# The third MLP stage of a fused transformer block, computed with its features on the partitions

## The chip, the cores and the metric

The kernel runs on one core of one Trainium2 chip. The time is that of the whole launch on the device, in microseconds (us), and is given as the median of several runs. A profile comes from one more execution. PE is TensorE, ACT is ScalarE, DVE is VectorE, POOL is GpSimd and SP is SyncE, which here only issues DMAs.

## What is computed

The input x has 8 groups of 512 rows with 256 features. Cut to what matters, the reference is:

```
y = LN(x)                                   # no weights
y = y + attention(LN(y; ln1))               # causal linear attention, 64 features
y = y + f2(gelu(f1(LN(y; ln2))))            # 256 -> 1024 -> 256
x = x + y
z = LN(x)                                   # no weights
h = gelu(z @ ternary(W_fc).T)               # 256 -> 1024, weights -1, 0, 1
h = LN(h; ln_w, ln_b)                       # over the 1024 features
out = x + h @ ternary(W_proj).T             # 1024 -> 256, weights -1, 0, 1
```

The last four lines are the third stage, which the change rewrites. The kernel never forms the normalised h. With w for ln_w, mean mu and deviation r of a row of h, out is x + r·(W(w·h) − mu·W(w)) + W(ln_b): it projects w·h, and takes the mean off behind the projection with a row vector W(w), `csum_b` in the code. W(ln_b) is `cpj_b`.

## The kernel before

Work is done in groups g = 0 to 7 of N = 512 rows, four tiles t of 128. D is 256, the hidden width H is 1024. A matrix with features on the partitions has KD = 2 or KH = 8 blocks of 128, counted by m. A float32 value is kept as the sum of two rounded parts, hi and lo; a full product takes three matmuls (`split3`, L261), a product with exact ternary weights two. ACT writes the hi part from PSUM, DVE the lo part as PSUM − hi. PSUM has eight banks of 512 float32 per partition: bank_f (2), bank_y (2), bank_a (2), bank_p, bank_q.

Each engine runs a list of calls that is written out by hand (`first`, `step(g)`, `last` in each engine's block), and engines wait for each other's semaphores. Steps of up to three groups are interleaved. For a group they are:

- LN1 and attention: `tu`, `qk_mm`, `scores`, `v_mm`, `attend` on PE (L338 to L419), then LN2 and the transposes `tz2` (L421).
- `f1` (L428): eight calls m of six matmuls of 512 columns into bank_f[m % 2]; `gelu` (L758) on ACT in place, `h_hi` (L765) on ACT, `h_lo` (L1121) on DVE. `f2` (L450) adds 12 matmuls of 256 columns per m into bank_y, rows on the partitions; in the last group `f2h` (L461) does it by halves of the rows.
- LN3: `y_sum` (L1128), `ln3_stats` and the variance on DVE, `ln3_rstd` (a power) on POOL, `ln3_shift` on DVE, `z3_norm` on ACT, then the transposes `tz3` (L467), `z3_hi` (ACT), `z3_lo` (DVE).
- Stage 3: `fc(g, t, c)` (L477): rows on partitions, four matmuls of 512 columns into bank_f[c], eight calls. `gelu3` (L784) writes h into the SBUF buffer h3. `ln4_stats` (L1153) takes mean and variance per row on DVE with bn_stats. `tr(g, h, q)` (L494), eight calls, turns two blocks m of two tiles into bank_y[q % 2]. `g_hi` (L793, ACT) and `g_lo` (L1165, DVE) split them, scaled with w, 128x256 each. `proj` (L523, `last_proj` L508) takes 8 matmuls of 256 columns per call, two tiles (one half h) at a time into bank_p.
- `correct` (L1387, POOL) adds −mu·r·csum_b to yc, which holds x + cpj_b (`y_cpj`, L1377), and `output` (L1174, DVE) adds r times the projection. SP stores halves of a group.

The setup in the first 60 us loads and splits the weights, and finds the ternary ones (`threshold`, `ternary` L930).

## Time and profile before

| | us |
|---|---|
| median of 3 runs (lowest, highest) | 457.57 (457.09, 457.77) |
| span of the profiled execution | 455.2 |
| PE busy | 437.5 |
| DVE busy | 367.7 |
| ACT busy | 310.7 |
| POOL busy | 238.6 |

The span goes from the first to the last instruction of the profiled execution; its own time as a run is not listed, so the median stands beside it, 2.4 us longer. Instructions, DMA issues and waits are not counted as busy. A matmul's listed duration includes the pipeline behind it: two in a row overlap, and what one costs in the queue is read from start to start.

### The profile page before, as it was taken

The page shows a single profiled execution, that of the slowest core. Times are in us where ns is not written, and L with a number is a line of the kernel's source. Part 1 is how long each engine was busy: PE and PEld are TensorE (multiplying, and loading weights), DVE is VectorE, ACT ScalarE, POOL GpSimd, SP SyncE. Part 2 cuts the span into 40 slices and gives each one's busy share as a digit, 9 for nine tenths or more (in the row PEclk, how much of TensorE's full clock was granted, in tenths as well). Part 3 has the DMA queues.
Part 4 walks back from the last instruction along what each step waited for, and adds up shares of the span by engine and source line. Part 5 has one row for each costly group of instructions (what it writes and reads, how often), then busy time and mean ns, then how long its engine had stood idle before and what let it go on. Part 6 is the DMA issues. An engine that isn't in the chain of part 4 may idle for free.

```text
span 455.2 us, 8867 instructions
## 1 busy us (share of the span) xinstructions
PE 437.5 (96%) x2942; PEld 395.5 (87%) x2942; DVE 367.7 (81%) x1200; ACT 310.7 (68%) x580; POOL 238.6 (52%) x224
## 2 busy tenths in 40 slices
PE   3898999999989999999999999999999999999997
PEld 3786897889978899889998999889988899888986
DVE  6899989877968878888788879888799837867596
ACT  4887937895188855878668855779468854786173
POOL 3887215843358517682549525694496225181334
PEclk9999999999999999999999999999999999999999
DMA  7234010120111201030101201021100000000001
GB/s 241 118 99 181 0 49 1 48 71 1 9 62 48 69 3 48 34 102 6 48 25 48 69 2 46 25 70 48 48 24 1 24 1 1 25 1 24 0 25 48
DMA packets 13518, 20.41 MB, mean 45 GB/s; under 512 B 2720, under 2 KB 11040, under 8 KB 12960
## 3 DMA queue, kind: packets, MB, share of 16 engines
q1 hardware_dynamic: 13472, 19.84, 13.3%
q8 instruction: 24, 0.39, 0.3%
q14 instruction: 22, 0.18, 0.1%
HBM read 15.62 MB, written 4.22 MB: 44 GB/s over the span
## 4 chain that ended last, share of the span: by engine, by line
PE 76%; DVE 7%; issue 7%; POOL 4%; DMA 3%; ACT 1%; SPq 1%; POOLq 0%; DVEq 0%
PE bank_f L490 11%; PE bank_p L538 10%; PE bank_f L263 6%; PE bank_f L265 6%; PE bank_f L264 6%; PE bank_y L263 6%; PE bank_y L264 6%; PE bank_y L265 6%; PE bank_y L504 5%; PE bank_a L263 4%; PE bank_a L265 4%; PE bank_a L264 4%; DMA h<-in_f 2%; PE bank_a L271 1%; PE bank_f L271 1%
## 5 line engine op out<-in xcount | busy, mean ns | idle before, releaser
L1334 POOL TENSOR_TENSOR rs<-ve,neg_half 128x2 f32<-128x2 f32 x48 | 33.6, 702 | 134.1 <-DVE ve L972 131.2
L763 ACT ACTIVATE bank_f<-bank_f,f_bias 128x512 f32<-128x512 f32 x64 | 42.3, 660 | 37.8 <-PE bank_f L265 36.9
L263 PE MATMUL bank_y<-wf_hi,h_hi 128*128 128x256 f32 x240 | 67.2, 280 | 0.0
L264 PE MATMUL bank_y<-wf_lo,h_hi 128*128 128x256 f32 x240 | 67.1, 280 | 0.0
L265 PE MATMUL bank_y<-wf_hi,h_lo 128*128 128x256 f32 x240 | 67.1, 279 | 0.0
L1035 DVE TENSOR_TENSOR h_lo<-bank_f,h_hi 128x512 fp32r<-128x512 f32 x60 | 41.3, 688 | 29.9 <-ACT h_hi L771 29.5
L1170 DVE SCALAR_TENSOR_TENSOR g_lo<-bank_y,vec,g_hi 128x256 fp32r<-128x256 f32 x128 | 55.5, 478 | 10.7 <-ACT g_hi L800 10.2
L800 ACT ACTIVATE g_hi<-bank_y,vec 128x256 fp32r<-128x256 f32 x128 | 53.4, 479 | 12.0 <-PE bank_y L504 10.3
L538 PE MATMUL bank_p<-wpj_t,g_hi 128*128 128x256 f32 x240 | 60.0, 286 | 0.0
L538 PE MATMUL bank_p<-wpj_t,g_lo 128*128 128x256 f32 x240 | 58.6, 280 | 0.0
L263 PE MATMUL bank_f<-z2T_hi,wf_hi 128*128 128x512 f32 x128 | 52.4, 410 | 3.0 <-DVE h_lo L1035 1.9
L490 PE MATMUL bank_f<-wfc_t,z3T_hi 128*128 128x512 f32 x128 | 53.8, 420 | 0.6 <-DVE z3T_lo L1035 0.6
L265 PE MATMUL bank_f<-z2T_hi,wf_lo 128*128 128x512 f32 x128 | 50.8, 397 | 0.0
L490 PE MATMUL bank_f<-wfc_t,z3T_lo 128*128 128x512 f32 x128 | 50.6, 395 | 0.0
L264 PE MATMUL bank_f<-z2T_lo,wf_hi 128*128 128x512 f32 x128 | 50.6, 395 | 0.0
L791 ACT ACTIVATE h<-bank_f 128x512 f32<-128x512 f32 x64 | 38.6, 604 | 14.5 <-PE bank_f L490 13.5
L263 PEld LDWEIGHTS bank_y<-wf_hi,h_hi 128*128 128x128 f32 x240 | 45.1, 188 | 1.3 <-issue 0.3
L538 PEld LDWEIGHTS bank_p<-wpj_t,g_hi 128*128 128x128 f32 x240 | 45.1, 188 | 1.1
L538 PEld LDWEIGHTS bank_p<-wpj_t,g_lo 128*128 128x128 f32 x240 | 45.2, 188 | 1.1
L264 PEld LDWEIGHTS bank_y<-wf_lo,h_hi 128*128 128x128 f32 x240 | 45.1, 188 | 1.0
L265 PEld LDWEIGHTS bank_y<-wf_hi,h_lo 128*128 128x128 f32 x240 | 45.1, 188 | 0.0
L1156 DVE BATCH_NORM_STATS2 bn<-h 128x6 f32<-128x512 f32 x64 | 40.9, 681 | 0.0
(299 smaller groups left out, 1227.7 us busy)
## 6 DMA issues: line engine op xcount, KB each, us to landing
out<-y_yc SPq DMA_DIRECT2D x15, 256.0 KB, 2.2
u<-in_xt SPq DMA_DIRECT2D x6, 512.0 KB, 3.7
lines_b<-lines SPq DMA_DIRECT2D x6, 512.0 KB, 3.9
x_even<-in_x SPq DMA_DIRECT2D x8, 256.0 KB, 2.9
x_odd<-in_x SPq DMA_DIRECT2D x8, 256.0 KB, 3.1
h<-in_f SPq DMA_DIRECT2D x1, 1024.0 KB, 7.7
y_yc<-in_f SPq DMA_DIRECT2D x1, 1024.0 KB, 10.0
h<-in_fc SPq DMA_DIRECT2D x1, 1024.0 KB, 4.8
```

What stands on the lines that cost most here:

```text
L263: pe.matmul(ps, w[0], r[0], start=start, stop=False, skip_group_check=skip)
L264: pe.matmul(ps, w[0], r[1], start=False, stop=False, skip_group_check=skip)
L265: return pe.matmul(ps, w[1], r[0], start=False, stop=stop, skip_group_check=skip)
L490: mm = pe.matmul(bank_f[c][:], z3T[part][:, k, t * P:(t + 1) * P], wfc[:, k, c * 512:(c + 1) * 512], start=(k == 0 and part == 0), stop=(k ...
L538: mm = pe.matmul(bank_p[:, t * D:(t + 1) * D], gr[part][:, (8 * g + 4 * h + q) % RG, i, t * P:(t + 1) * P], wpj[:, m, :], start=(m == 0 an ...
L763: act.activation(bank_f[m % 2][:], bank_f[m % 2][:], ACT.Gelu, bias=f1_bias[:, m:m + 1]).then_inc(s["h_gelu"], 1)
L791: act.activation(h3[:, t, c * 512:(c + 1) * 512], bank_f[c][:], ACT.Gelu).then_inc(s["h3_ready"], 1)
L800: act.activation(gr[0][:, n % RG, i, :], bank_y[q % 2][:, i * D:(i + 1) * D], ACT.Copy, scale=ln3w_c[:, m:m + 1]).then_inc(s["g_hi"], 1)
L1035: dve.tensor_tensor(dst, b, hi.bitcast(F32), ALU.subtract).then_inc(s[ready], 1)
L1156: dve.bn_stats(bn[3][:, t, 6 * c:6 * c + 6], h3[:, t, c * 512:(c + 1) * 512]).then_inc(s["ln4_bn"], 1)
L1170: dve.scalar_tensor_tensor(gr[1][:, n % RG, i, :], bank_y[q % 2][:, i * D:(i + 1) * D], ln3w_c[:, m:m + 1], gr[0][:, n % RG, i, :].bitcast ...
L1334: pool.tensor_tensor(rs[n][:, 2 * h:2 * h + 2], ve[n][:, 2 * h:2 * h + 2], neg_half[:, 0:2], ALU.pow).then_inc(s[f"ln{n + 1}_rs"], 1)
```

## The change

Stage 3 keeps its features on the partitions from fc to proj.

- `fc(g, m)` takes the weights block m as the stationary operand and moves the 512 rows: bank_f[m % 2] then holds features m by rows. For m = 0 and 1 it is cut into halves of 256 rows (`fch`), and so is f1 (`f1h`). No transpose of h is needed.
- `gelu3` works in place in PSUM. ACT's `g_hi` and `square` and DVE's `g_lo` (which waits for both) read the bank from there, 512 columns each.
- `proj(g, m)` moves 258 columns: the weights block of 256, and two more that hold 1/w as hi and lo. A tile's 257th and 258th results add up to the sum of h over the features. Its four tiles lie in bank_y[0], bank_y[1], bank_p and bank_a[0], so f2 of the next group waits for `centre`.
- POOL adds the eight squared blocks (`sq_add`, seven per group), PE transposes the sum (`tsq`), DVE sums over it (`h2_sum`).
- DVE makes mean and variance from the two sums (`h_sum`, `ln4_var`) and takes the mean off each tile (`centre`); POOL does rstd once per group and `output` (two multiplications, two additions); in the last group DVE's `last_output`.
- 1/w needs w ≠ 0: where w is 0, 1 is used in its place and the row of the projection weights is masked (`used_weights` on DVE, `wpj_mask` on POOL, `inv_hi` and `inv_lo`).
- All call lists are written anew, one `order()` per engine; the stores of SP come half 1 before half 0 in groups 1 to 4 and 6.

The core of it, with one row of the lists:

```diff
-        wpj = sb("wpj_t", [P, KH, D], F32R)
+        wpj = sb("wpj_t", [P, KH, D + 2], F32R)
...
+        def out_bank(t):
+            return (bank_y[0], bank_y[1], bank_p, bank_a[0])[t]
...
+            def fc_wait(g, m):
+                if g == G - 1 and m < 2:
                     pe.wait_ge(s["h_lo"], 8 * G)
...
+                if m >= 2:
+                    pe.wait_ge(s["g_lo"], 8 * g + m - 1)
+                    pe.wait_ge(*squared(g, m - 2))
+
+            def fc_mm(m, cols):
                 for k in range(KD):
                     for part in range(2):
-                        mm = pe.matmul(bank_f[c][:], z3T[part][:, k, t * P:(t + 1) * P], wfc[:, k, c * 512:(c + 1) * 512],
+                        mm = pe.matmul(bank_f[m % 2][:, cols], wfc[:, k, m * P:(m + 1) * P], z3T[part][:, k, cols],
                                        start=(k == 0 and part == 0), stop=(k == KD - 1 and part == 1))
...
+            def proj(g, m):
+                pe.wait_ge(s["g_lo"], 8 * g + m + 1)
...
+                for t in range(T):
+                    for part in range(2):
+                        mm = pe.matmul(out_bank(t)[:, 0:D + 2], gr[part][:, (8 * g + m) % RG, t * P:(t + 1) * P],
+                                       wpj[:, m, :], start=(m == 0 and part == 0), stop=(m == KH - 1 and part == 1))
...
+            def tsq(g):
...
+                for t in range(T):
+                    mm = pe.transpose(bank_a[1][:, t * P:(t + 1) * P], squares[:, 0, t * P:(t + 1) * P], ident[:])
...
+            def gelu3(g, m):
+                act.wait_ge(s["fc_done"], 8 * g + m + 1)
+                act.wait_ge(s["fc_half"], 2 * g + min(m, 1) + 1)
+                act.activation(bank_f[m % 2][:], bank_f[m % 2][:], ACT.Gelu).then_inc(s["h3_ready"], 1)
...
+            def square(g, m):
...
+                act.activation(squares[:, m, :], bank_f[m % 2][:], ACT.Square).then_inc(squared(g, m)[0], 1)
...
+            def g_lo(g, m):
+                n = 8 * g + m
+                dve.wait_ge(s["g_hi"], n + 1)
+                dve.wait_ge(*squared(g, m))
...
+            def h_sum(g):
...
+                for t in range(T):
+                    dve.wait_ge(s["pj_tile"], 4 * g + t + 1)
+                    dve.tensor_reduce(h_total[:, t:t + 1], out_bank(t)[:, D:D + 2], AXX, ALU.add).then_inc(s["h_total"], 1)
...
+                dve.scalar_tensor_tensor(centred[:, t, :], csum_b, h_mean[:, t:t + 1], out_bank(t)[:, 0:D],
+                                         ALU.mult, ALU.add).then_inc(s["centred"], 1)
...
+            def sq_add(g, m):
...
+                pool.tensor_tensor(squares[:, 0, :], squares[:, 0, :], squares[:, m, :], ALU.add).then_inc(s["squares_sum"], 1)
...
+                f2(7, 6, 0); f2(7, 7, 0); f2(7, 5, 1); f2(7, 6, 1); f2(7, 7, 1); tz3(7, 0); tz3(7, 1); fch(7, 0, 0)
```

Three places of the engines' queues follow. Names left of the arrow are written, those right of it read. The first is PE at the seam of group 2, where v_mm of group 3 (into bank_a from wvo) ends and the transposes tz3 of group 2 (into bank_f from z) begin; L538 is proj, v_hi and ae_hi belong to attend. Before:

```order
L265 MATMUL bank_a<-wvo_hi,uT_lo 128x256
L538 MATMUL bank_p<-wpj_t,g_hi 128x256
L538 MATMUL bank_p<-wpj_t,g_lo 128x256
...
L263 MATMUL bank_a<-v_hi,ae_hi 128x258
L265 MATMUL bank_a<-v_hi,ae_lo 128x258
L538 MATMUL bank_p<-wpj_t,g_hi 128x256
L538 MATMUL bank_p<-wpj_t,g_lo 128x256
...
L263 MATMUL bank_a<-v_hi,ae_hi 128x258
...
L271 MATMUL bank_f<-ident,z 128x128 x4
```

And with the change:

```order
L287 MATMUL bank_a<-wvo_lo,uT_hi 128x256
L288 MATMUL bank_a<-wvo_hi,uT_lo 128x256
L294 MATMUL bank_f<-ident,z 128x128 x8
L286 MATMUL bank_a<-v_hi,ae_hi 128x258
L287 MATMUL bank_a<-v_lo,ae_hi 128x258
...
L288 MATMUL bank_a<-v_hi,ad_lo 128x258
L519 MATMUL bank_f<-z3T_hi,wfc_t 128x256
L519 MATMUL bank_f<-z3T_lo,wfc_t 128x256
```

The proj calls between v_mm and the transposes are gone, and both tz3 come directly behind v_mm, ahead of attend(3, 0) and attend(3, 1), after which the first fc halves (L519) follow.

The second is ACT at the start of stage 3 of the same group. Before (h is the gelu's result in SBUF):

```order
L791 ACTIVATE h<-bank_f 128x512
L662 ACTIVATE z<-xa,sh,rs 128x256 x2
L791 ACTIVATE h<-bank_f 128x512 x3
L800 ACTIVATE g_hi<-bank_y,vec 128x256 x2
L756 ACTIVATE z2T_hi<-bank_a 128x2x256
L791 ACTIVATE h<-bank_f 128x512
L800 ACTIVATE g_hi<-bank_y,vec 128x256 x2
L791 ACTIVATE h<-bank_f 128x512
```

With the change (h now holds the squares, bank_f<-bank_f is the gelu):

```order
L805 ACTIVATE z3T_hi<-bank_f 128x2x256 x2
L765 ACTIVATE v_hi<-bank_a 128x2x256
L810 ACTIVATE bank_f<-bank_f 128x512
L824 ACTIVATE g_hi<-bank_f,w_used 128x512
L836 ACTIVATE h<-bank_f 128x512
L810 ACTIVATE bank_f<-bank_f 128x512
L836 ACTIVATE h<-bank_f 128x512
L824 ACTIVATE g_hi<-bank_f,w_used 128x512
L716 ACTIVATE uT_hi<-u 128x2x256
L810 ACTIVATE bank_f<-bank_f 128x512
```

Gelu no longer leaves the bank; each m has three ops on it, and the copies and squares stand in alternating order.

The third is DVE at the end of the program. Before:

```order
L1170 SCALAR_TENSOR_TENSOR g_lo<-bank_y,vec,g_hi 128x256 x2
L978 TENSOR_SCALAR sh<-mv,rs 128x1 x2
L972 TENSOR_SCALAR ve<-mv 128x1 x2
L1170 SCALAR_TENSOR_TENSOR g_lo<-bank_y,vec,g_hi 128x256 x4
L978 TENSOR_SCALAR sh<-mv,rs 128x1 x2
L1170 SCALAR_TENSOR_TENSOR g_lo<-bank_y,vec,g_hi 128x256 x4
L1184 SCALAR_TENSOR_TENSOR y_yc<-bank_p,rs,y_yc 128x256 x2
L1184 SCALAR_TENSOR_TENSOR y_yc<-bank_a,rs,y_yc 128x256 x2
```

With the change:

```order
L1263 SCALAR_TENSOR_TENSOR g_lo<-bank_f,w_used,g_hi 128x512 x8
L1221 TENSOR_REDUCE h_total<-bank_a 128x4
L1231 TENSOR_REDUCE h_total<-bank_y 128x1 x2
...
L1236 SCALAR_TENSOR_TENSOR h_mean<-h_total 128x4
L1241 SCALAR_TENSOR_TENSOR ve<-h_total,h_mean 128x4
L1243 TENSOR_SCALAR ve<-ve 128x4
L1251 TENSOR_SCALAR h_mean<-h_total 128x4
L1256 SCALAR_TENSOR_TENSOR centred<-pj_rows_b,h_mean,bank_y 128x256 x2
L1256 SCALAR_TENSOR_TENSOR centred<-pj_rows_b,h_mean,bank_p 128x256
L1271 SCALAR_TENSOR_TENSOR y_yc<-centred,rs,y_yc 128x256 x2
L1256 SCALAR_TENSOR_TENSOR centred<-pj_rows_b,h_mean,bank_a 128x256
L1271 SCALAR_TENSOR_TENSOR y_yc<-centred,rs,y_yc 128x256 x2
```

Statistics stood among the g_lo steps; now the sums, the variance and the centring all follow the last g_lo, and the outputs close the queue.

## Rows read from the trace of the kernel before

**Rows 1.** Page, busy time, share of the span and instructions of each engine
```profile
PE 437.5 (96%) x2942; PEld 395.5 (87%) x2942; DVE 367.7 (81%) x1200; ACT 310.7 (68%) x580; POOL 238.6 (52%) x224
```

**Rows 2.** Stretches: us, busy and instructions by engine, clock, DMA share, GB/s
```profile
0.00:72.30 72.30, 60.18 (x375) 52.33 (x375) 63.16 (x202) 50.61 (x90) 37.10 (x41) 1.00 0.31 108
...
180.04:231.90 51.86, 51.86 (x360) 47.64 (x358) 42.87 (x145) 37.30 (x69) 29.87 (x27) 1.00 0.13 42
...
430.00:455.20 25.20, 21.85 (x152) 19.56 (x151) 19.26 (x58) 12.28 (x26) 9.25 (x9) 1.00 0.10 33
```

**Rows 3.** Waits: engine, out, line, releaser: us, times, longest
```profile
PE bank_a L279 <- DVE less_w L891: 7.1, 1, 7.1
```

**Rows 4.** Timeline of PE, stage 3 of group 2: start, us, engine, line, operation
```profile
185.22 0.60 PE L504 MATMUL bank_y<-ident,h 128*128 128x128 f32 x4
185.58 0.48 PE L490 MATMUL bank_f<-wfc_t,z3T_hi 128*128 128x512 f32 x1
185.90 0.40 PE L490 MATMUL bank_f<-wfc_t,z3T_lo 128*128 128x512 f32 x1
186.13 0.39 PE L490 MATMUL bank_f<-wfc_t,z3T_hi 128*128 128x512 f32 x1
```

**Rows 5.** Groups by form: count, busy us and mean ns, idle before
```profile
L504 PE MATMUL bank_y<-ident,h 128*128 128x128 f32 x256 | 37.8, 272 | 0.0
L1156 DVE BATCH_NORM_STATS2 bn<-h 128x6 f32<-128x512 f32 x64 | 40.9, 681 | 0.0
L800 ACT ACTIVATE g_hi<-bank_y,vec 128x256 fp32r<-128x256 f32 x128 | 53.4, 479 | 12.0 <-PE bank_y L504 10.3 <-PE bank_p L538 1.6
L1396 POOL TENSOR_TENSOR y_yc<-y_yc,mean_part 128x512 f32<-128x512 f32 x16 | 20.9, 1303 | 1.2
L708 ACT ACT_TABLE_LOAD x7 | 9.0, 1283 | 0.1
```

**Rows 6.** Timeline of PE, 256 and 258 columns, first and twelfth call
```profile
213.02 0.28 PE L263 MATMUL bank_y<-wf_hi,h_hi 128*128 128x256 f32 x1
...
214.32 0.28 PE L265 MATMUL bank_y<-wf_hi,h_lo 128*128 128x256 f32 x1
...
230.08 0.28 PE L263 MATMUL bank_a<-v_hi,ae_hi 128*128 128x258 f32 x1
...
231.42 0.28 PE L265 MATMUL bank_a<-v_hi,ad_lo 128*128 128x258 f32 x1
```

**Rows 7.** Timeline of ACT, stage 3 and f1 of the middle
```profile
185.42 0.60 ACT L791 ACTIVATE h<-bank_f 128x512 f32<-128x512 f32 x1 [0.77 <-PE bank_f L490]
185.91 0.84 ACT L800 ACTIVATE g_hi<-bank_y,vec 128x256 fp32r<-128x256 f32 x2
...
195.06 0.66 ACT L763 ACTIVATE bank_f<-bank_f,f_bias 128x512 f32<-128x512 f32 x1 [0.27 <-PE bank_f L265]
195.75 0.60 ACT L771 ACTIVATE h_hi<-bank_f 128x512 fp32r<-128x512 f32 x1
```

**Rows 8.** Timeline of DVE and ACT after group 7's last f2 half
```profile
430.49 0.69 DVE L1136 TENSOR_TENSOR y_yc<-bank_y,y_yc 128x512 f32<-128x512 f32 x1 [0.84 <-PE bank_y L265]
...
433.38 0.34 DVE L978 TENSOR_SCALAR sh<-mv,rs 128x1 f32<-128x1 f32 x2 [0.81 <-POOL rs L1334]
...
433.79 0.60 ACT L662 ACTIVATE z<-y_yc,sh,rs 128x256 f32<-128x256 f32 x1 [0.84 <-DVE sh L978]
```

**Rows 9.** Timeline of the last DVE step, and of a 128x4 rstd on POOL
```profile
451.55 0.88 DVE L1184 SCALAR_TENSOR_TENSOR y_yc<-bank_a,rs,y_yc 128x256 f32<-128x256 f32 x2 [0.15 <-POOL y_yc L1396]
...
202.25 1.04 POOL L1328 TENSOR_TENSOR rs<-ve,neg_half 128x4 f32<-128x4 f32 x1
```

**Rows 10.** Timeline of DVE in the setup, and a group of small ones
```profile
39.60 1.73 DVE L939 TENSOR_SCALAR y_yc<-h,theta 128x1024 f32<-128x1024 f32 x1
...
48.13 0.74 DVE L939 TENSOR_SCALAR y_yc<-h,theta 128x1024 f32<-128x1024 f32 x1
...
L956 DVE TENSOR_SCALAR few_rows<-mean_w,select 4x128 f32<-4x128 f32 x2 | 1.5, 774 | 0.0
```

More of the change, by code:

```diff
@@ L325, in cpj @@
                 for k in range(KH):
[L326 removed]
+                    mm = pe.matmul(bank_p[0:4, 0:D], ln3_split[:, k, :], wpj[:, k, 0:D],
                                    start=(k == 0), stop=(k == KH - 1))
@@ L533, in proj @@
                         pe.wait_ge(s["spread_ready"], 1)
-                for i in range(2):
-                    m = 2 * q + i
-                    for t in range(2):
-                        for part in range(2):
-                            mm = pe.matmul(bank_p[:, t * D:(t + 1) * D],
-                                           gr[part][:, (8 * g + 4 * h + q) % RG, i, t * P:(t + 1) * P], wpj[:, m, :],
-                                           start=(m == 0 and t == 0 and part == 0), stop=(m == KH - 1 and part == 1),
-                                           skip_group_check=True)
@@ L604, in _ @@
+            order()
         @block.scalar
@@ L861, in _, with pj_wait @@
-            first()
-            for g in range(1, 4):
-                step(g)
-            last()
+            def gelu3(g, m):
+                act.wait_ge(s["fc_done"], 8 * g + m + 1)
+                act.wait_ge(s["fc_half"], 2 * g + min(m, 1) + 1)
+                act.activation(bank_f[m % 2][:], bank_f[m % 2][:], ACT.Gelu).then_inc(s["h3_ready"], 1)
+            def pj_wait(n):
+                act.wait_ge(s["pj_tile" if n % KH == 0 else "pj_done"], n // KH * 4 if n % KH == 0 else n - n // KH)
@@ L866, in _ @@
+            order()
         @block.vector
@@ L1261, in _, with h2_sum @@
-            first()
-            for g in range(1, 4):
-                step(g)
-            last()
+            def h2_sum(g):
+                dve.wait_ge(s["sq_done"], g + 1)
+                if g:
+                    dve.wait_ge(s["ln4_ve"], g)
+                dve.tensor_reduce(h2_total[:], bank_a[1][:].rearrange("p (t f) -> p t f", t=T),
+                                  AXX, ALU.add).then_inc(s["h2_total"], 1)
+            def h_sum(g):
+                if g:
+                    dve.wait_ge(s["h_mean"], g)
+                    dve.wait_ge(s["h_mean2"], g)
+                for t in range(T):
+                    dve.wait_ge(s["pj_tile"], 4 * g + t + 1)
+                    dve.tensor_reduce(h_total[:, t:t + 1], out_bank(t)[:, D:D + 2], AXX, ALU.add).then_inc(s["h_total"], 1)
@@ L1266, in _ @@
+            order()
         @block.gpsimd
```

777 lines of the change are left out of this document (420 added, 357 removed).

## The prediction

> **What bounds the kernel now.** I read the page's busy times first. TensorE (PE) is busy 437.5 of 455.2 us; the others have a fifth to a half of the span to spare [rows 1]. Then the table by stretch, to see whether that holds everywhere. In the middle it does: a group takes 51.9 us and PE is busy for all of it, at a granted clock of 1.00 (2.4 GHz), while DVE, ACT and POOL work 42.9, 37.3 and 29.9 us of it. Of PE's 17.7 idle us, 12.1 lie in the first 72.3 us and 3.35 in the last 25.2 [rows 2]; 2.3 are left for all between. So in the middle only PE work counts, and a wait for another engine costs nothing until it is longer than the matmuls that the order puts beside it. Most of the idle time at the start is one wait for the setup weights, 7.1 us [rows 3], which the change leaves.
>
> **What leaves PE.** The stretch of rows inside a group shows what a transposing call of stage 3 costs in the queue. Its four transposes start at 185.22 and the next matmul at 185.58, which then takes .32 us to the following start instead of .23: .36 + .09, so .44 us [rows 4]. Eight calls a group (256 transposes in all [rows 5]) are 3.5 us a group. The new tsq(g), four transposes of the squares' sum, brings one such call back: −.44. The projection keeps 64 matmuls a group, now 258 columns wide. Twelve calls of 256 columns go .118 us apart ((214.32 − 213.02)/11), twelve of 258 columns .122 ((231.42 − 230.08)/11) [rows 6]; that would be .26 us a group. Two columns at the pace of a 512-column matmul, .23/512, are .06 us a group. I take .13, between the two. The fc matmuls keep their columns: 32 × 512, or 24 × 512 and 16 × 256 where m = 0 and 1 are cut in halves, at the same pace per column within .01 us. Net 2.95 us a group, 23.6 us in all. PE work falls from 437.5 to 413.9 us, 48.9 per group.
>
> If nothing else changed, that alone would give 457.57 − 23.6 = 434 us. The rest of this part is what takes it back.
>
> **The other engines.** DVE loses bn_stats (64 in 40.9 us) and some small steps, and 128 g_lo of 256 columns become 64 of 512; it falls to about 35 us a group. ACT has 64 gelu (.66), 64 scaled copies (.69 at most) and 64 squares (.60) of 512 columns for 64 gelu (.60) and 128 copies (.48, 53.4 in all) [rows 5, 7]: 125 for 92 us, 4.1 a group more, some 41 us. In the queue it is less per op: two independent ops of 512 columns start .49 us apart, an op that needs the one before it .69 us after it [rows 7]. With about .09 more for a scale column (an estimate from those two) gelu, copy and square take .65 + .57 + .50, near 1.7 us per m. POOL gains seven adds of 128x512 (the kind of L1396, 1.30 us each [rows 5]), and its four correction steps become four output steps: 29.9 + 9.1, 39 us. SP's stores and loads change places, but all DMAs use 13% of the engines in a group [rows 2], and the steps that refill yc have a whole group's time: nothing. All three stay under 48.9, so none bounds by its sum.
>
> **The new chain inside stage 3.** The third stage now works in two PSUM banks in turn. In each, the next fc may start only when the bank was read by g_lo and square: fc .93, some .20 to the release, gelu .65, copy .57, square .60 where it starts late, g_lo .69 and .1 to PE. That is 3.75 us per bank and round, 1.87 us per m, 15 us for eight. In the same stretch PE has 16.4 us of work (fc 7.5, seven proj at .98, tz2 and part of attend), so on paper it is covered. But the cover is uneven: the first two m have only attend beside them, and ACT also has z2_norm and z2_hi there. Nothing in the trace prices this. The bounds are nothing (covered) and 1.87 (one m exposed); I charge a third of that, .6 us a group, as the cover is 1.4 us in all: 4.2 for seven groups. Before, a bank was free after gelu alone, and transposes and proj lay between.
>
> **The seam between f2 and fc.** Before, in the order, proj(g−1) and attend stood between v_mm and tz3; now proj is done earlier, and in groups 1 and 2 tz3 comes straight after v_mm. The chain after the last f2 can be read in the last group: y_sum starts at 430.49, released by the f2 that ended some .2 before; statistics, variance and POOL's rstd follow, the shift ends at 433.72 and ACT's z at 434.39 [rows 8], 4.1 us in all. v_mm is 24 matmuls, 2.9 us, and v_hi stands before z3_norm on ACT (.4 more), so tz3 is late by some 1.6 us in groups 1 and 2; with one or two attends (.4 to .7 us) in between, .5 in groups 3 to 6, and in group 0 (v_mm, cpj and spread first) .2. Sum 5.4. The start of f2 now waits for centre(g−1), because proj's results lie in f2's banks: after the last proj some 3 us of sums and centre steps on DVE, beside it 2.8 us of f1(g, 2) and (g, 3); .3 a group, 2.1. Two masks of wpj on POOL, 2.6 us each by L1396's pace, stand before the first proj and may cost nothing or 2.6: 1, as fc lies beside them. Groups 0 to 6 idle 12.7 us, where they idled 2.3.
>
> **Start.** selectors, ln3_lo and the ternary steps stand elsewhere on DVE and the first scores after v_mm. A gain of 4 us and a loss of 1 are the bounds, since the 7.1 us wait stays: I take 2, 10 us idle.
>
> **The end.** Before, the last f2 ends at about 430.3 [rows 8] and the span 24.9 us later, with PE nearly full, because f2 half 0 was finished first and fc already ran. Now f2(7,7,1) closes the queue for tz3(7,1), and nothing stands behind it. Counted from the last f2: z at 4.1, tz3 to 4.5, z3_hi 5.1, z3_lo 5.8; half 0 is through earlier and its half of fc runs in that wait, as if the whole fc had started at 5.3. With fc .93 and .2 the first gelu starts at 6.4, the eighth seven rounds of 1.87 later, at 19.5. Its gelu and square (1.25) and POOL's add (1.3) end at 22.2 with the hand-over; tsq(7) and then the last proj follow on PE, 1.8 us with releases: 24.0. Then four sums, mean and variance (1.0), rstd of 128x4 on POOL 1.04 us [rows 9], and one centre step and the four outputs behind it (five of .44): 28.4. From the last DVE op's end to the span's end went 2.8 us (451.55 + .88 = 452.43 [rows 9]); that makes 31.2. PE works 16.4 us of it and idles 14.8.
>
> **Sum.** 413.9 + 10 + 12.7 + 14.8 = 451.4 us of span. The three runs before have a median of 457.57, 2.4 over the profiled span; adding the same, **453.8 us**. The removal is worth 23.6 us, and all but 3.8 is given back.
>
> **A rule against the change.** POOL is to be busy for 39 of 49 us a group. Its work seems to slow DVE ops that read SBUF alone: the compare of 128x1024 took 1.73 us at 39.60 and .74 at 48.13, and ops of 4x128 average .77 us [rows 10]. h_mean, the variance and the first small sums are such ops. The Trainium skill, "GPSIMD Engine Reference", section "Key points", says that POOL shares its SBUF interfaces with VectorE and contends with DVE instructions in a 2-port mode or with two SBUF inputs. By that rule, centre and f2 behind it would come later, which is the third case below; the sum above has no charge for it.
>
> **Rivals and chances.** A measurement of this kernel can tell about 0.2% from no change, 456.7 to 458.5 us.
> - *Stalls take most of it* (my forecast, 449 to 456.6), 0.45.
> - *The stalls are covered.* PE is full at 51.9 us with the orders as they stand, so a new order may well be full too [rows 2]. Groups 0 to 6 would idle 4, the start 12, the end 14.8: 413.9 + 30.8 + 2.4 = 447.1. Against it: the bank now waits for three readers. 0.15.
> - *Contention by POOL.* Four small DVE ops per group at .7 in place of .15 us are 2.2 us in the chain to centre, of which matmuls of f1 may hide three quarters; .5 us a group shows, 4 in all, giving 457.8, no change. 0.15.
> - *The two-bank round sets the pace* (slower). If ACT reaches each bank .2 us later than I assume (a z2_norm or u_hi in front, a square that cannot start beside the copy), four rounds a bank add .8 us a group, 8 groups 6.4 us: 460.2. For it: 1.87 against a PE supply of 2.05 us per m is a cover of a tenth only, and tz2, z2_norm and z2_hi fall into it. Against: ACT had 14 us free per group [rows 2]. From .47 us more per group than I charged (3.8/8) the gain is gone, and from .59 the change is slower by over 0.2%. 0.25.
> - *Square needs a table of its own.* A load takes 1.28 us [rows 5]; two for each of 64 m are 160 us on ACT. The program's order holds 14 loads on ACT, before 16, so I leave it no chance.
>
> The range takes in the covered case but for its tail, and the last case up to a little over its centre, so that some 0.1 of it is left out: 446 to 461.5 us; faster 0.60, same 0.15, slower 0.25.
>
> **What would show it.** Right: PE's busy time near 414 and, per middle group, 1.5 to 2.5 us of PE idle time, released by g_lo or square (fc, f1) and z3_lo; the stretch from the last f2 to the end near 31 us with PE busy about half of it. Covered: a period of 49 us. Contention: h_mean and ve of .6 us or more, PE waiting for centred. Rounds: PE waits for g_lo at nearly every fc, period over 51.9. Wrong altogether: DVE or POOL with no idle time in a group, or PE's busy time near 437, which would mean that the pitch of 258 columns or of the wide matmuls is not as read here; or a granted clock under 1.00, which would raise every PE term.

## The result: 468.8 us, slower by 2.3%

| | before | after |
|---|---|---|
| median of 4 runs (lowest, highest), us | 457.67 (457.09, 459.0) | 468.8 (466.49, 469.22) |
| span of the profiled execution | 455.2 | 467.3 |
| its own time | not listed | 469.05 |

The ratio is 1.0233, with a 95% interval of 1.0205 to 1.0262. The forecast of 453.8 us and its range both miss, and on the wrong side. The page of the changed kernel, its busy times and PE's clock in 40 slices:

```profile
PE 428.6 (92%) x2878; PEld 386.6 (83%) x2878; DVE 327.9 (70%) x1027; ACT 329.3 (70%) x579; POOL 306.5 (66%) x270
...
PEclk9899899999999999999999999999999999999799
```

PE is busy 8.9 us less than in [rows 1], not 23.6. That number deceives: a matmul's listed duration holds the pipeline behind it, so that after each wait some idle time is listed as busy, and at half clock a matmul is listed longer (.41 us in place of .28 for 256 columns). I therefore give every matmul its pitch from start to start at full clock (.2335 us for 512 columns, .117 for 256, .120 for 258, .109 for a transpose), and call the sum **PE's work** and all else **idle**. Work is 425.0 us before and 402.2 after: 22.8 us were removed, as forecast (23.6). The idle time by stretch:

| PE idle, us | before | after | more | forecast |
|---|---|---|---|---|
| start to the first fc (72.3; 78.7) | 20.1 | 27.2 | +7.1 | −2.1 |
| from there to the end of the last f2 (430.3; 434.3) | 6.0 | 21.4 | +15.4 | +10.4 |
| from there to the end (24.9 us; 33.0 us) | 4.2 | 16.6 | +12.4 | +11.4 |

(The forecast counted its idle time against PE's listed busy time; the column gives its differences to [rows 2] as it read them: 12.1, 2.3 and 3.35.) Together 34.9 us are lost and 22.8 gained: +12.1, the 467.3 − 455.2 of the spans. (The median is 1.5 us over the span here and was 2.4 over it before, so the medians differ by 11.1.) The stretches of the changed kernel (us, busy time and instructions by engine, clock, DMA share, GB/s) are the start, one middle group, and the end, as in [rows 2]:

```profile
0.00:78.70 78.70, 61.36 (x382) 53.94 (x382) 63.12 (x208) 47.84 (x89) 41.42 (x44) 0.96 0.30 100
183.40:237.00 53.60, 52.22 (x359) 47.13 (x358) 38.20 (x122) 39.78 (x70) 38.97 (x34) 1.00 0.13 41
434.30:467.30 33.00, 20.66 (x118) 17.43 (x116) 16.09 (x43) 16.48 (x29) 16.18 (x14) 0.86 0.10 33
```

No engine is full. The granted clock, 1.00 in all of [rows 2], is .96 and .86 in two of these stretches. (The trace has no clock record before 12.1 us in the kernel before and 11.2 in the changed one, and the views count that time as 1.00. PE goes at half pace there in both: the transposes from 7.99 on are .21 us apart in the kernel before, twice their pitch.)

**The start.** PE's and DVE's timelines (start us, us, engine, line, operation, idle before and releaser):

```profile
18.55 0.77 PE L286 MATMUL bank_p<-uT_hi,wqk_hi 128*128 128x512 f32 x1 [4.32 <-DVE wqk_lo L924]
48.98 0.79 PE L286 MATMUL bank_f<-z2T_hi,wf_hi 128*128 128x512 f32 x1 [2.27 <-DVE h_lo L1101]
```

```profile
13.79 0.75 DVE L1051 BATCH_NORM_STATS2 bn<-x_odd 128x6 f32<-128x256 f32 x2 [4.71 <-DMA x_odd<-in_x]
...
15.05 1.28 DVE L1106 SCALAR_TENSOR_TENSOR uT_lo<-bank_f,uT_hi 128x512 fp32r<-128x512 f32 x2
16.25 2.16 DVE L924 SCALAR_TENSOR_TENSOR wqk_lo<-qk_relu,vec,wqk_hi 128x128 fp32r<-128x128 f32 x2
```

DVE's new list puts ln1_stats(1, 0), which needs a DMA, ahead of u_lo and wqk_lo, which the first qk product needs: that product starts at 18.55, against 12.45 before. In the stretch behind the gap PE runs at half clock:

```profile
18.50:21.40 2.90, 2.85 (x7) 2.30 (x8) 1.94 (x9) 0.60 (x1) 2.82 (x4) 0.50 0.00 0
```

The second gap above, 2.3 us ahead of 48.98, has half clock about its end again, from 48.7 to 52.1. There PE waits for an h_lo that stands on DVE behind two ternary steps, 3.5 us together (44.74 to 48.2); before, the same pair of steps left PE a gap of 1.41 us. The loss of 7.1 us is nearly made up of these: a gap of 4.3 us that was not there, .9 more in the second, and about 1.4 us of pace lost in each half clock stretch, less the .9 us by which PE's first product comes sooner.

**The middle.** PE's waits (us in total, times, longest), of which before knew only the second, with 1.7 us:

```profile
PE bank_f L519 <- DVE g_lo L1263: 6.6, 11, 1.0
...
PE bank_f L294 <- ACT z L683: 5.7, 7, 3.1
...
PE bank_y L286 <- DVE centred L1256: 0.7, 2, 0.4
```

The second includes the 3.1 us ahead of the last group's end. The same waits end PE's weight loads too, so some more is hidden under PEld. By what came next after an excess over the pitch, the five periods from 130.5 to 392.3 lose 8.2 us ahead of or inside fc, 3.5 at the seam (tz3 2.3, attend 1.2), 2.6 in f2, 1.2 in f1, 1.1 in scores and proj. A period is 52.4 us: 49.0 of work and 3.3 idle. Before it was 52.1: 51.6 and .5.

**The end.** The wait ahead of tz3(7, 0) is 3.08 us, and then the clock is halved:

```profile
437.52 0.84 PE L294 MATMUL bank_f<-ident,z 128*128 128x128 f32 x4 [3.08 <-ACT z L683]
438.62 1.09 PE L294 MATMUL bank_a<-ident,z 128*128 128x128 f32 x4 [0.26 <-DVE z L1082]
439.87 0.55 PE L519 MATMUL bank_f<-z3T_hi,wfc_t 128*128 128x256 f32 x1 [0.16 <-DVE z3T_lo L1101]
440.21 0.41 PE L519 MATMUL bank_f<-z3T_lo,wfc_t 128*128 128x256 f32 x1
440.43 0.41 PE L519 MATMUL bank_f<-z3T_hi,wfc_t 128*128 128x256 f32 x1
```

fc's 256 columns are .21 us apart here; in the middle .12. The table by stretch:

```profile
437.80:444.70 6.90, 5.74 (x24) 4.44 (x22) 2.41 (x4) 4.02 (x8) 1.79 (x2) 0.51 0.23 80
```

### The profile page after: what moved, and what is told of

Its sections match the earlier page's. It is cut to its first block and busy times, and to the rows that moved or that the text cites. A ratio compares the mean times of both kernels' runs of the same rounds, so it can differ in the third digit from the quotient of the medians.

```text
span 467.3 us, 8905 instructions
## 1 busy us (share of the span) xinstructions
PE 428.6 (92%) x2878; PEld 386.6 (83%) x2878; DVE 327.9 (70%) x1027; ACT 329.3 (70%) x579; POOL 306.5 (66%) x270
## 5 line engine op out<-in xcount | busy, mean ns | idle before, releaser
L1443 POOL TENSOR_TENSOR h<-h 128x512 f32<-128x512 f32 x56 | 72.4, 1292 | 14.9 <-issue 7.5
L1263 DVE SCALAR_TENSOR_TENSOR g_lo<-bank_f,w_used,g_hi 128x512 fp32r<-128x512 f32 x64 | 47.9, 749 | 46.2 <-ACT h L836 24.4
L519 PE MATMUL bank_f<-z3T_hi,wfc_t 128*128 128x512 f32 (+1 forms) x160 | 58.6, 379 | 7.1 <-DVE g_lo L1263 6.6
L286 PE MATMUL bank_f<-z2T_hi,wf_hi 128*128 128x512 f32 (+1 forms) x160 | 57.9, 362 | 3.4 <-DVE h_lo L1101 2.5
L288 PE MATMUL bank_f<-z2T_hi,wf_lo 128*128 128x512 f32 (+1 forms) x160 | 56.4, 352 | 0.0
L287 PE MATMUL bank_f<-z2T_lo,wf_hi 128*128 128x512 f32 (+1 forms) x160 | 56.3, 352 | 0.0
L519 PE MATMUL bank_f<-z3T_lo,wfc_t 128*128 128x512 f32 (+1 forms) x160 | 55.0, 355 | 0.0
L810 ACT ACTIVATE bank_f<-bank_f 128x512 f32<-128x512 f32 x64 | 37.7, 589 | 11.8 <-PE bank_f L519 11.0
L824 ACT ACTIVATE g_hi<-bank_f,w_used 128x512 fp32r<-128x512 f32 x64 | 43.8, 687 | 1.3 <-PE bank_a L548 0.4
L519 PEld LDWEIGHTS bank_f<-z3T_hi,wfc_t 128*128 128x128 f32 x160 | 31.1, 194 | 15.8 <-DVE g_lo L1263 11.8
```

The source lines that it names most:

```text
L286: pe.matmul(ps, w[0], r[0], start=start, stop=False, skip_group_check=skip)
L287: pe.matmul(ps, w[0], r[1], start=False, stop=False, skip_group_check=skip)
L288: return pe.matmul(ps, w[1], r[0], start=False, stop=stop, skip_group_check=skip)
L519: mm = pe.matmul(bank_f[m % 2][:, cols], wfc[:, k, m * P:(m + 1) * P], z3T[part][:, k, cols], start=(k == 0 and part == 0), stop=(k == KD ...
L810: act.activation(bank_f[m % 2][:], bank_f[m % 2][:], ACT.Gelu).then_inc(s["h3_ready"], 1)
L824: act.activation(gr[0][:, n % RG, :], bank_f[m % 2][:], ACT.Copy, scale=w_used[:, m:m + 1]).then_inc(s["g_hi"], 1)
```

## Experiments

Each ratio is to the kernel before, run beside that version on the same chip (medians 456.9 to 457.67), so differences of some tenths between rows of the table mean nothing. Each run's idle time is from its own profiled execution, by the pitches above: start to the first fc; the first fc of group 0 to that of group 6; the end from the last f2 (the whole length, in brackets the idle time in it; the filling of e4_fill counts as work).

| run | median, us | ratio, 95% interval | start | middle | end |
|---|---|---|---|---|---|
| before | 457.67 | | 20.1 | 5.6 | 24.9 (4.2) |
| the change | 468.8 | 1.0233, 1.0205–1.0262 | 27.2 | 19.7 | 33.0 (16.6) |
| b1_nocover | 468.65 | 1.0253, 1.0236–1.027 | 19.7 | 17.8 | 25.0 (4.2) |
| b2_tail | 464.07 | 1.0149, 1.0125–1.0172 | 20.7 | 5.6 | 31.3 (10.5) |
| e1_start | 466.32 | 1.019, 1.0158–1.0222 | 22.9 | 19.6 | 34.8 (18.4) |
| e5_setup | 467.25 | 1.0228, 1.0212–1.0243 | 25.5 | 19.2 | 33.2 (16.8) |
| e9_setup2 | 464.65 | 1.0169, 1.0145–1.0192 | 22.3 | 20.0 | 33.2 (16.7) |
| e4_fill | 467.32 | 1.0227, 1.0202–1.0253 | 26.8 | 19.4 | 33.5 (14.3) |
| e6_tail | 473.24 | 1.0352, 1.0304–1.0399 | 27.0 | 19.9 | 35.1 (19.0) |
| e2_nosq | 460.29 | 1.0047, 1.0015–1.0078 | 27.4 | 17.0 | 32.1 (16.1) |
| e8_noadd | 466.6 | 1.0207, 1.0192–1.0222 | 26.3 | 18.5 | 33.0 (16.6) |
| e3_sqsb | 477.8 | 1.0477, 1.0409–1.0545 | 26.3 | 26.1 | 34.3 (17.8) |
| e11_gfirst | 469.28 | 1.027, 1.025–1.0291 | 26.2 | 20.1 | 34.4 (17.9) |
| e12_z2dve | 472.37 | 1.0311, 1.0292–1.033 | 23.8 | 25.2 | 33.3 (16.9) |
| e13_z2none | 465.75 | 1.0177, 1.0147–1.0208 | 23.7 | 19.7 | 33.1 (16.7) |
| e14_z2nosq | 457.81 | 1.0018, 1.0002–1.0034 | 22.3 | 18.4 | 31.2 (15.2) |

### The start: e1_start, e5_setup, e9_setup2

e1_start, in DVE's list:

```diff
-                u_odd(0, 1); ln1_stats(1, 0); u_lo(0, 0)
-                u_lo(0, 1); wqk_lo(); qk_bias_add(); wvo_add(); ln1_stats(1, 1)
+                u_odd(0, 1); wqk_lo(); qk_bias_add(); u_lo(0, 0)
+                u_lo(0, 1); ln1_stats(1, 0); wvo_add(); ln1_stats(1, 1)
```

> Only DVE's list is changed: ln1_stats(1, 0) comes behind wqk_lo, qk_bias_add and the two u_lo of group 0. After the change DVE waited 4.7 us for x_odd there, with these steps queued behind it, PE's first qk product started at 18.55 us in place of 12.45, and PE's clock stood at half from 18.0 to 21.4 us. If this queue is the loss at the start, the qk product starts near 14 to 14.5, that stretch of half clock is gone, and the time falls by 4 to 6 us, to 463 to 465. Rival: the start is bound by the weights' arrival and by the later waits (h_lo at 48.98), and less than 1.5 us come back.

The first qk product started at 13.87, the first fc came at 74.4, 4.3 us sooner, and the first half clock stretch was gone; the second stayed (45.0 to 48.4). The time fell by only 2.5 us, between what was expected and the rival: behind the last f2 the clock stayed at half from 434.1 to 444.4, 3.4 us longer than in the change, for no edit there.

e5_setup puts the calls of all engines up to tz3(0, ·) in the old kernel's order; e9_setup2 besides moves two calls of POOL:

```diff
-                n1o(1); ln1_rstd(2, 0); ln1_rstd(2, 1); x_mul(2, 0); ln3_rstd(0, 0)
-                ln3_rstd(0, 1); x_mul(2, 1)
+                n1o(1); ln1_rstd(2, 0); ln1_rstd(2, 1); ln3_rstd(0, 0); ln3_rstd(0, 1)
+                x_mul(2, 0); x_mul(2, 1)
```

> The change with the setup's call lists of before on PE, DVE, ACT and POOL, up to the second v_mm of group 1 (used_weights and inv_hi added among them, one gelu_table call more); from tz3(0, 0) on everything as with the change. If the order of the setup alone makes its start late, the first fc comes at 72 to 73 us in place of 78.7, no stretch of half clock is left before 60 us, and the time is 462 to 463.5. Rival: the new work of the setup (used_weights, halves of f1) costs some of it, and the first fc comes at 75 or later; then 465 or more.

> As e5_setup (the setup's lists of before), and on POOL the two ln3_rstd of group 0 stand ahead of x_mul(2, 0). In e5_setup PE came to tz3(0, 0) 6 us sooner, at 68.6 us, and then waited 4.6 us: POOL's x_mul(2, 0) waited for its DMA until 69.5 and took 1.5, with ln3_rstd behind it. If the loss at the start is only which step stands behind a wait for a DMA, the first fc comes at 72 to 73.5, the half clock at 73.4 is gone, and the time falls to 462 to 463.5. Rival: another wait takes its place, and the time stays over 465.

e5_setup brought PE to tz3 of group 0 some 6 us sooner, where it lost most of that again, so that the first fc came at 77.0 and the time was the rival's, though not for the rival's reason. PE and POOL in it:

```profile
73.26 2.10 PE L294 MATMUL bank_f<-ident,z 128*128 128x128 f32 x8 [4.46 <-ACT z L719]
```

```profile
69.54 1.51 POOL L1500 TENSOR_TENSOR u<-u,lines_b 128x512 f32<-128x512 f32 x1 [7.35 <-DMA lines_b<-lines]
```

x_mul(2, 0) waited 7.4 us for a DMA with ln3_rstd(0, ·) queued behind it, and z of group 0 needs that rstd. With the two changed round (e9_setup2) the first fc comes at 73.8, and 4.1 us of the change's 11.1 are back, about 1 us less than was expected. In the change itself the x_mul cost nothing yet, since everything was late already: it was through at 69.9, and the ln3_rstd behind it then waited for DVE.

```profile
73.55 0.71 POOL L1419 TENSOR_TENSOR rs<-ve,neg_half 128x2 f32<-128x2 f32 x1 [3.61 <-DVE ve L1038]
```

So of the 7.1 us that PE idles more at the start, 4.9 are order, with the clock that dropped in the gaps: ln1_stats(1, 0) in front of what the first qk product needs (e1_start), then the rest of the setup's lists. x_mul in front of ln3_rstd is a second trap that shows once the first is gone. The other 2.2 us stay in e9_setup2, which waits 1.8 us at tz3 of group 0; their cause was not tested.

### The cover at the seam: b1_nocover

The kernel before with three calls of proj a group moved ahead of the last f2, as the changed kernel must do it (its results lie in f2's banks). No work is added:

```diff
-                scores(g + 2); f2(g + 1, 4); f1(g + 1, 7)
+                scores(g + 2); proj(g, 1, 1); proj(g, 1, 2); proj(g, 1, 3); f2(g + 1, 4); f1(g + 1, 7)
...
-                v_mm(g + 2, 0); v_mm(g + 2, 1); proj(g, 1, 1)
-                attend(g + 2, 0); proj(g, 1, 2); attend(g + 2, 1); tz3(g + 1, 0)
+                v_mm(g + 2, 0); v_mm(g + 2, 1)
+                attend(g + 2, 0); attend(g + 2, 1); tz3(g + 1, 0)
```

> The kernel before, with one edit of PE's list: in groups 2 to 6 the three proj calls of the group before (1, 1) to (1, 3) that stood between v_mm and fc stand behind scores instead, ahead of the rest of f1 and f2. Nothing else changes, no work is added. If those calls cover the LN3 chain, PE waits .6 to 1.5 us at tz3 and fc in each of five groups, and the time rises by 3 to 7 us, to 460 to 464: that much of the change's loss in the middle would be the lost cover. If v_mm and attend cover the chain alone, the time stays within 1 us of 457.5.

It is as slow as the change, which is chance: it has all of the old PE work and none of the losses at the start and the end. It is also 5 us slower than was expected. PE's waits in it; the first was 1.7 us in the kernel before, the third .6, the second not among the listed:

```profile
PE bank_f L271 <- ACT z L662: 3.6, 7, 0.6
PE bank_a L263 <- DVE v_lo L1035: 3.1, 2, 2.2
PE bank_f L490 <- DVE z3T_lo L1035: 2.1, 5, 0.6
```

The middle idles 12.2 us more: 1.3 to 1.9 in each of three groups, which is near what was expected, and 4.6 and 2.5 in the last two, where attend waits for v_lo and the clock falls once (342.0 to 345.4). So the chain from f2 to fc was there before, hidden in part behind these 24 matmuls (2.8 us). The other engines' lists were left as they were, and the v_lo part comes of lists that were made for the other order. The change, whose lists were made for its own order, loses far less at this place (3.5 us in five groups), so this run shows that the calls were cover; it does not say what their loss cost the change.

### Stage 3, ACT or POOL: e2_nosq, e8_noadd, e12 to e14

e2_nosq leaves out squares, their sum and its transposes, and makes the variance from a constant. e8_noadd leaves out POOL's adds alone.

```diff
             def square(g, m):
+                return
...
             def sq_add(g, m):
+                return
```

> Leaves out the squares: ACT's square, POOL's sq_add and PE's tsq are gone, the sum of squares is a constant. The four transposes of tsq are .44 us a group, 3.5 in all. If the two-bank round of stage 3 (gelu, copy, square, g_lo) makes PE's idle time in the middle (2.9 us a group over that of before, by start to start), a round is .5 to .6 us shorter per bank, the middle period falls from 52.4 to about 50 us, and the last round takes about 1.4 us per m in place of 1.94 (4 us less at the end); in all 468.8 falls by 3.5 + 8 + 4, to 451 to 455. If the idle time comes from elsewhere (seams, the order, DVE), only tsq and some of the end come back: 461 to 465.

> Leaves out POOL's sq_add alone (the variance is then that of one block's squares): ACT still squares and g_lo, fc and f1 still wait for it, tsq still runs. 9 us of POOL work per group are gone. If POOL's load slows DVE's small SBUF ops and so the start of f2, h_mean (128x4) falls from .43 to .17 us at the median, ve likewise, and 1 to 3 us come back (466 to 468). If the bank's readers on ACT and DVE are all that counts, nothing comes back before the last group, and the end gains at most .5 us: 468 to 469.

Without squares ACT has 4.8 us less a group (eight of .595), and idles 2.6 to 4.3 us between the first and the eighth gelu, where it idled .6 to .75 in five of groups 1 to 6. Yet PE's idle time in the middle falls by 2.7 us of 19.7 only. The time, 460.29 us, is just under what was expected if the two-bank round is not the cause (461 to 465). The span is 7.4 us shorter: 3.5 of PE work, the 2.7, 1.1 ahead of the last group's end and .5 in it, less .2 at the start. Without the adds alone the middle gains 1.2 us; of the 2.2 us in all, .9 lie in the start, which this edit leaves alone, so that the 466.6 fits the expectation for POOL's load in its time, but only about half of it in its place.

e12_z2dve (with e9_setup2's start) moves the odd tiles of z2 from ACT to DVE, as z2_odd behind ln2_shift in DVE's list; e13_z2none writes one column of them; e14_z2nosq is e13 and e2 together, so both leave work out.

```diff
-                pair(z, xa, 1, h, 0, "z2_ready", g == 0)
+                pair(z, xa, 1, h, 0, "z2_ready", True)
```

> The start order of run e9_setup2, and besides in every group the two odd tiles of the second norm (z2, [128x256] scaled and shifted by ACT, about .5 us each) are computed by DVE, so that some 1.0 us of ACT's work per group leaves the stretch in which ACT is also to serve gelu, copy and square. DVE gets 1.0 us per group more, with room for it. Theory A (ACT paces stage 3, since it is busy for all but .7 us of it): the stretch from the first to the eighth gelu falls from about 15.2 to 14.3 to 14.8 us and the idle time of PE between the groups falls by 2 to 5 us; time 460 to 463 (e9_setup2: 464.65). Theory B (PE's queue without cover, or the hand-over of the two banks, sets the pace and ACT's being busy is a result of it): the groups keep a period near 52.3 us, PE idles as before; time 464 to 465.5.

> As e12_z2dve, but the two odd tiles of the second norm are left out in groups 1 to 7 (DVE writes one column of each, some .15 us), so the stage behind them reads old values there; ACT has 1.0 us less per group, DVE nothing more. Theory A (ACT's work paces stage 3): first to eighth gelu 14.1 to 14.4 us against 15.2, PE's idle time in the middle 3 to 6 us below e9_setup2's 20.0, time 459 to 462. Theory B (the hand-over through DVE's g_lo and the banks paces it): stage 3 stays within .3 us of 15.2, ACT idles over 1.5 us in it, time 464 to 465.5. Theory C (the order lacks cover elsewhere: f2, tz3, attend): stage 3 gets shorter, but PE's idle time turns up elsewhere, middle idle falls by under 2 us, time 463 to 464.5.

> As e13_z2none, and the squares, their sum and its transposes are left out too (the variance is made from a constant), as in e2_nosq: ACT has 5.8 us less per group than the change, POOL 9 us less. Theory A: PE stalls in fc nearly vanish, the middle idles under 12 us (e2_nosq 17.0, e9_setup2 20.0), time 452 to 455. Theory C: what is left idle does not depend on ACT's or POOL's work, the middle keeps 15 to 18 us as in e2_nosq, time 456 to 459 (e2_nosq 460.29 with the slower start, some 3 us).

e12_z2dve was 7.7 us slower than e9_setup2, 5.2 of it in the middle: outside both expectations. DVE's group of z2_odd and PE's wait for g_lo:

```profile
L1153 DVE TENSOR_SCALAR z<-xa,rs,sh 128x256 f32<-128x256 f32 x16 | 13.8, 862 | 0.6
```

```profile
PE bank_f L518 <- DVE g_lo L1336: 11.9, 19, 1.2
```

Each is .86 us on DVE, twice a group, ahead of a g_lo that PE waits for; in e13_z2none, with the same relief for ACT and none of this, the row reads

```profile
PE bank_f L518 <- DVE g_lo L1340: 6.6, 12, 1.2
```

like that of the change. There ACT idles 1.1 to 1.7 us in stage 3 (2.8 in group 2), but the stage lasts 15.1 to 15.5 us as before (16.8 in group 2, as before too) and the middle idles 19.7: theory A falls, and of the other two it is theory B that had a stage of the same length. e14_z2nosq bears out that A falls: its time (457.81) is in the range of theory C, its middle (18.4) just over it (15 to 18). B and C are not told apart by these runs; they name the same waits from two sides, the bank's way back and the place in PE's queue where nothing lies beside it. The middle in the change, and in it:

```profile
78.70:392.30 313.60, 305.04 (x2100) 277.36 (x2099) 224.45 (x713) 238.66 (x416) 224.94 (x193) 1.00 0.11 35
```

```profile
73.80:383.40 309.60, 301.44 (x2076) 274.64 (x2075) 220.24 (x720) 211.23 (x356) 173.21 (x152) 1.00 0.12 35
```

ACT works 27 and POOL 52 us less, and PE still idles 18.4 against 19.7 us. What PE loses in the middle hangs on neither engine's sum of work. What is left is the chains that PE's queue leaves uncovered; no run gave the changed kernel its cover back, so this is read from the trace. They show one by one: the fc of m = 2, the first that needs a bank back, starts .43 to 1.07 us late in five of groups 1 to 6, since attend alone lies between (in group 2 it is a later fc, 1.17). Group 4 of the change:

```profile
291.96 0.28 PE L288 MATMUL bank_a<-v_hi,ad_lo 128*128 128x258 f32 x1
293.15 0.50 PE L519 MATMUL bank_f<-z3T_hi,wfc_t 128*128 128x512 f32 x1 [0.91 <-DVE g_lo L1263]
...
295.15 0.40 PE L519 MATMUL bank_f<-z3T_hi,wfc_t 128*128 128x512 f32 x1
```

From there on, fc and proj fill PE for 1.9 us per m. ACT's gelu, copy and square take 1.76 to 1.78 back to back (the gelu at 298.94 to the next at 300.72), but the second norm's z and z2T_hi and the next group's uT_hi stand among them, and together they leave ACT only .6 to .75 us idle: the two engines are level.

### The bank's readers: e3_sqsb, e11_gfirst

e3_sqsb squares g_hi from SBUF in place of the bank, with g_hi ahead of square in ACT's list, so that fc no longer waits for square. The sum is then that of other squares than the reference's. e11_gfirst is the order alone.

```diff
-                act.activation(squares[:, m, :], bank_f[m % 2][:], ACT.Square).then_inc(squared(g, m)[0], 1)
+                act.wait_ge(s["g_hi"], 8 * g + m + 1)
+                act.activation(squares[:, m, :], gr[0][:, (8 * g + m) % RG, :].bitcast(F32), ACT.Square).then_inc(squared(g, m)[0], 1)
```

> ACT's square reads the copy g_hi in SBUF (so it squares w times h) in place of the bank, and stands behind the copy everywhere; fc, f1 and g_lo no longer wait for it. ACT, POOL and PE do the same work as with the change, but a bank has two readers behind gelu. If the serial readers of the bank make the stalls, 5 to 9 us come back (460 to 464), nearly as much as the squares' removal gives beyond tsq. If ACT's own work (1.8 us per m) is the pace, nearly nothing comes back at the end (last round still 1.9 us per m) and under 3 us in all (466 to 468).

> The change with ACT's copy g_hi ahead of the square for every m (27 of 64 pairs swapped), all waits kept. e3_sqsb had this order and read the square from SBUF, and was 9 us slower than the change. If the order did that (the square then delays g_lo and the next gelu at the wrong places), this one is slower too, 472 to 478. If reading the square from SBUF did it, this one is within 2 us of 468.8.

The miss of the study: 9 us slower, where a reader less should have helped. ACT in the last group of e3_sqsb:

```profile
452.11 0.69 ACT L822 ACTIVATE g_hi<-bank_f,w_used 128x512 fp32r<-128x512 f32 x1
452.91 0.63 ACT L835 ACTIVATE h<-g_hi 128x512 f32<-128x512 f32 x1
453.45 0.58 ACT L808 ACTIVATE bank_f<-bank_f 128x512 f32<-128x512 f32 x1
```

The square starts .80 us behind the copy whose result it needs, .11 after its end; an independent op follows .50 to .59 behind. That is some .2 us for each m; the first to the eighth gelu take 16.0 to 17.7 us in place of 14.9 to 16.8, and the middle idles 6.4 us more. So ACT's pace stands just at PE's: taking work off ACT brings little, adding to it costs at once. The order alone costs nothing that can be told (469.28 against 468.8).

### The end: e4_fill, e6_tail, b2_tail

e4_fill puts 12 matmuls of 512 columns, whose result nobody reads, into the last gap; e6_tail finishes half 0 of the last group first, as the old kernel did; b2_tail takes that head start from the kernel before, on PE and ACT (shown: PE).

```diff
-                f2(7, 7, 1); tz3(7, 0); tz3(7, 1); fch(7, 0, 0)
+                f2(7, 7, 1); keep(12); tz3(7, 0); tz3(7, 1); fch(7, 0, 0)
```

```diff
-                f2(7, 6, 1); f2(7, 7, 1); tz3(7, 0); tz3(7, 1); fch(7, 0, 0)
-                fch(7, 0, 1); fch(7, 1, 1); fch(7, 1, 0)
+                f2(7, 6, 1); tz3(7, 0); f2(7, 7, 1); fch(7, 0, 0); fch(7, 1, 0); tz3(7, 1)
+                fch(7, 0, 1); fch(7, 1, 1)
```

```diff
-                f2h(7, 7, 1); fc(7, 0, 0); fc(7, 0, 1); proj(6, 1, 2); fc(7, 1, 0); proj(6, 1, 3); tz3(7, 1)
+                f2h(7, 7, 1); tz3(7, 1); fc(7, 0, 0); fc(7, 0, 1); proj(6, 1, 2); fc(7, 1, 0); proj(6, 1, 3)
```

> Twelve matmuls of 512 columns on operands at hand, into bank_p, stand between the last f2 and tz3(7, 0), where PE idled 3.1 us and the granted clock then fell to half from 437.85 to 444.7 us. If the idle time is what lets the clock fall, it stays at 1.00 there; the transposes and the first fc halves take half the time, the first gelu starts about 1.8 us sooner after the last f2, and the time falls by 1.5 to 2 us, to about 467. Rival: the clock falls anyway, or the fill delays tz3; then no gain or a loss of up to .5.

> The change with another order in the last group: all half 0 calls of f2 before the half 1 calls, tz3(7, 0) ahead of the last f2, and the half 0 parts of fc for m = 0 and 1 behind it, with DVE and ACT taking LN3 half by half. If the bare wait for half 1's chain is what costs, the first gelu comes at 6.3 to 6.8 us after the last f2 in place of 8.2, and the time falls by 1.5 to 2 us (467). Rival: as with the fill, the clock falls later instead and the gain is under .5 us.

> The kernel before, with tz3(7, 1) on PE and z3_norm(7, 1), z3_hi(7, 1) on ACT ahead of fc(7, 0, 0), gelu3(7, 0, 0): fc of half 0 then waits until LN3 of half 1 is through, as the change's fc with 512 rows must. Nothing else is edited. The chain from the last f2 to z is 4.1 us: if the start of fc on half 0 alone is what keeps before's end short (24.9 us from the last f2, against 33.0 with the change), the end is 3 to 5 us longer, 460.5 to 462.5. Rival: other steps bound that end, and it is under 1 us longer.

With the fill, the first gelu came 7.2 us after the last f2 in place of 8.2, but the clock halved later, for 3.4 us from 444.8, and the end was no shorter in the profiled run, which took 468.86. The other three took 467.3, as expected; no trace shows where they gained. e6_tail was slower by 4.4 us, which neither expectation had. It had half clock for 10.2 us, 441.3 to 451.5, its first gelu at 8.7, and f2 waited 2.6 us more ahead of the end. b2_tail is the price of a late start in numbers: the end grows from 24.9 to 31.3 us, with half clock from 432.9 to 439.7 as a part of it; without the clock in mind, 3 to 5 us were expected. PE there:

```profile
434.97 1.11 PE L271 MATMUL bank_a<-ident,z 128*128 128x128 f32 x4 [3.99 <-ACT z L672]
435.74 0.78 PE L490 MATMUL bank_f<-wfc_t,z3T_hi 128*128 128x512 f32 x1
```

A fc with rows on the partitions can finish for half 0 while half 1 is still in f2; with features on the partitions gelu and all behind it need both halves. Of the 8.1 us that the change's end is longer, the head start's 6.4 would be most. That the chain of rounds on two banks is the rest was not tested.

No version beat the kernel before, and the one that comes level with it, e14_z2nosq, leaves work out.

## Why the prediction was wrong

- **What leaves PE** held: −22.8 for −23.6. The pitch of 258 columns was .120, the middle of the two readings.
- **Start** was the step that failed most: "a gain of 4 us and a loss of 1 are the bounds … I take 2". It was a loss of 7.1, 9.2 us off the forecast, which alone turns the forecast gain of 3.8 us into a loss of 5.4. I took the bounds from PE's old waits and from which calls had left, and did not ask of each call that had moved ahead what it waits for. e1_start shows it: ln1_stats(1, 0) stands in front of the first qk product behind a DMA, a gap of 4.3 us, and the fix brings the first fc 4.3 us sooner. e9_setup2 takes 4.9 of the 7.1 us back by order alone. The sentence also had the 7.1 us wait as one that stays; it is the wait for PE's first instruction, and it fell to 6.3.
- **The new chain inside stage 3** had the mechanism and too small a size. "I charge a third of that, .6 us a group"; around fc 1.6 a group were lost (8.2 / 5), a value near the upper bound of 1.87. "On paper it is covered" was a sum over eight m, while the first two m have attend alone beside them. The round itself was read well: 1.94 us in the last group, where I had 1.87, and gelu, copy and square back to back 1.76 to 1.78 where I had "near 1.7".
- **The seam and f2.** 5.4 and 2.1 were charged for seven groups. At the seam the charge held group by group: 1.5 us in groups 1 and 2 where 1.6 was charged, .5 to .6 in groups 3 to 6 where .5 was. f2 was charged too little: f2, f1 and scores lost 4.4 in the five middle periods (3.8 without scores), about 6 for seven, against 2.1.
- **The end** was right in its parts: idle +12.4 for +11.4. Of 33.0 us for 31.2, 1.8 arise ahead of the first gelu (8.2 after the last f2, not 6.4), where fc runs at half clock; from the first gelu to the end it is 24.8, as forecast (31.2 − 6.4), and by its parts too: 13.6 us to the eighth gelu for 13.1, 17.7 to the end of the last proj for 17.6. That e4_fill, at full clock there, had its first gelu at 7.2 says that the clock is about 1 of the 1.8 us.
- **Rivals.** *Covered* was wrong. *Contention by POOL* exists: the second 128x4 step of h_mean (L1251) takes .43 us by the median in the change, up to 1.15, and .17 in e2_nosq and e8_noadd, which have no adds. The other 128x4 steps stay at .16 by the median. But PE waited for centred .7 us in all, and e8_noadd has 2.2 us to gain; nothing near 4. The Trainium skill, "GPSIMD Engine Reference", section "Key points", names the shared SBUF interfaces; these rows agree that DVE ops slow down beside POOL, and no run shows which mode they ran in. *The two-bank round* had the sign and nearly the place, but e13_z2none and e14_z2nosq say that ACT's load is not what makes it late: with 1 and 5.8 us a group less on ACT the middle still idles 19.7 and 18.4 us.
- **The clock.** "A granted clock under 1.00" stood as what would make it wrong altogether. It fell for three short stretches while PE had work, 13.7 us together at half clock, and they account for about 3 us of the start's miss and some 1 of the end's 1.8.

The misses add up: start 9.2, middle 5.0, end .9, work .8 make the 15.9 us between the forecast span of 451.4 and 467.3. Against the median it is 15.0, since the 2.4 us that were added to the span came out as 1.5.

## What to carry to other kernels

Work that is taken from the bounding engine, or moved along its queue, may have been the cover of a chain: price the chain bare, at each place where the new order has nothing beside it, and not by the sum over a stage. Of every call that moves ahead of another on an in-order engine, ask which DMA or semaphore it waits for and who needs what stands behind it. A layout in which a stage can start on half of its input is worth its price at the end, where nothing else is left to run.
